# A three-layer graph network on one core: four record slots, pairs of tiles transposed with their numbers, features stored once

## The chip, the cores and the metric

The kernel runs on one core of a Trainium2 chip. The metric is the device time of one execution in microseconds (us); lower is better. The median of three runs of the kernel before is 3841.99 us.

## The reference, cut to what matters

```python
def reference(x, src, dst, edge_attr_16, We1, We2, Wn1, Wn2):
    # N, D, EF, L = 3125, 128, 16, 3 ; 100000 edges, each used in both directions
    s2, d2 = concatenate([src, dst]), concatenate([dst, src])
    ef2 = concatenate([ef, ef])
    h_prev = nf
    for l in range(L):
        e_in = concatenate([h_prev[s2], h_prev[d2], ef2], axis=-1)
        msg = leaky_relu(e_in @ We1[l]) @ We2[l]
        red = segment_sum(msg, d2, num_segments=N)
        n_in = concatenate([h_prev, red], axis=-1)
        out = leaky_relu(n_in @ Wn1[l]) @ Wn2[l]
        h_prev = out + h_prev
    return layernorm(x + out)
```

Each edge carries 16 features. Both directions of an edge share them.

## The kernel before

Three stages follow one another.

**Sort (0 to about 1122 us).** The edges are sorted by pairs of node blocks and written to the DRAM tensor `records`: 1152 tiles of 128 records, each of 34 float16 words (16 feature high halves, 16 low halves, and 2 numbers, the places of the edge's two nodes in their blocks).

**Reading the sorted records (about 1124 to 1284 us).** A batch is 32 tiles (`BATCH`), and two batches make one turn of the loop; 15 turns, so 30 batches, are live. `recc` has two slots, one for each batch of a turn. For a batch,
- GpSimd loads 272 KB of records into a slot (L644), once the batch two before it has been finished (`numT_set`, waited for at L643);
- TensorE transposes the features of each tile by itself (L1240: 32 transposes, 128x32 into 32x128, in four groups of eight, each to a bank of PSUM), and then the numbers of all 32 tiles in one more transpose (L1245);
- ScalarE copies two of the four groups to SBUF (L719) and VectorE the other two (L1018), 32x1024 each; VectorE also copies the numbers out of the records (L1011, L1013) and out of the last transpose (L1022). The copies of a batch with an even number go to `numb`, of an odd one to `gsel`, both free at this time;
- SyncE writes the features to the DRAM tensor `feat_d` twice (L529, two DMAs of 32 rows of 8 KB), so that it has 64 rows, and the numbers to `nums_d` (L532, 64 rows of 256 bytes).

At the end SyncE waits for these writes, copies the first part behind the last (L537, L538), and loads the first numbers and features of the next stage (L542, L546).

**Three layers (1319 to 2151, 2209 to 2970, 3025 to 3786 us).** Each runs 26 turns of 4 parts, a part is 3 steps, a step is 3 tiles. For each tile TensorE multiplies a tile of features (`fchunk`) with the weights `wst` (L1298), adds gathered node rows by four products with the one-hot matrix `gsel` (L1305), and after three steps adds the message to the sums by four products with `ssel`, a part of `loop_buf` (L1367, 12 for a step). ScalarE copies from PSUM (L750, L755) and makes the high half (L759); VectorE applies leaky relu (L1031) and makes the low half (L1101). In layer 0 VectorE also makes the one-hot matrices (L1035, L1118), and SyncE stores them to `gsel_d` and `ssel_d`; the other layers load them from there. There are 104 parts in a layer.

What sets the order around the change is SyncE's program, which issues one DMA after another:
- layer 0, for part p: wait until the gathers of the parts before p are done; load `fchunk` for part p+1 (L546: one DMA, 64 rows of 2304 bytes); wait for the one-hot matrix of part p+1; load numbers (L542), store `gsel` (L564), wait for the last `ssel` of part p, store it (L567);
- layers 1 and 2, for part p: wait until the sums of the steps before part p are done (`sum_done`); load `fchunk` for part p+1 (L546), `gsel` for part p+1 (L575), `ssel` for part p (L577).

TensorE waits in the first step of a part: for `fchunk` ahead of the first tile's feature product, for `gsel` ahead of its gathers, and for the `ssel` of the part before ahead of the third tile's feature product. `ssel` is thus loaded during the part just before the one that needs it.

`fchunk` rows 64 to 127 and `wst` rows 64 to 127 are set to zero once (L1037, L1038); `wst` is made anew in each layer (L1073 to L1079).

Of the kernel before, what the change touches and what calls it, by code (L numbers as in the profile page):

```python
# [23 lines left out]
P = 128  # L24
# [9 lines left out]
CHUNK = 8  # L34
# [8 lines left out]
TILES = 1152  # L43
# [7 lines left out]
assert TILES % (2 * BATCH) == 0  # L51
# [48 lines left out]
def build(nc, x, src, dst, ef, We1, We2, Wn1, Wn2, c_iota, c_part, c_tri, c_ident, c_tiles, c_steps, c_below, out):  # L100

    records = nc.dram_tensor("records", [TILES * P, RW], F16)
    feat_d = nc.dram_tensor("feat_d", [4 * EF, (TILES + PART) * P], F16)
# [8 lines left out]
    with ExitStack() as ctx:  # L112
# [105 lines left out]
        featT = [half[0:2 * EF, :, :].rearrange("p h e -> p (h e)")[:, 0:BATCH * P] for half in (numb, gsel)]  # L218
# [33 lines left out]
        recc = sb("recc", [P, 2, PREP, CHUNK, RW], F16)  # L252
        hrow = recc[:, :, :, :, :].rearrange("p k h t f -> p (k h t f)")[:, 0:2 * RUN * P].rearrange("p (h e) -> p h e", h=2)
        num16 = sb("num16", [P, 2, 2 * BATCH], F16)
        numT = sb("numT", [2 * BATCH, 2, P], F16)
# [17 lines left out]
        wc = sb("wc", [4 * EF, D], F32)  # L273
        wcs = sb("wcs", [4 * EF, D], F32)
        wch = sb("wch", [4 * EF, D], F16)
        wst = sb("wst", [P, 2, D], F16)
# [74 lines left out]
        recc_in = [sem(f"recc_in{h}") for h in range(2)]  # L351
        num16_set = sem("num16_set")
# [3 lines left out]
        numT_set = sem("numT_set")  # L356
        feat_out = [sem(f"feat_out{h}") for h in range(2)]
        nums_out = [sem(f"nums_out{h}") for h in range(2)]
# [58 lines left out]
        EDGE_DMAS, NODE_DMAS = 6, 2  # L417
# [26 lines left out]
        NUM_AHEAD = 2  # L444
        HIST_AHEAD = 2
        TR_STEPS = PREP + 1
# [4 lines left out]
        def _(sp):  # L451
# [11 lines left out]
            def load_edge_weights(l):  # L463
                sp.dma_start(wab[:, :, :], We1[ds(l, 1), 0:2 * D, :].rearrange("a (s k) f -> k (a s) f", s=2))\
                  .then_inc(w_in, DMA)
                for r in range(4):
                    sp.dma_start(wc[r * EF:(r + 1) * EF, :],
                                 We1[ds(l, 1), 2 * D:2 * D + EF, :].rearrange("a k f -> (a k) f")).then_inc(w_in, DMA)
# [14 lines left out]

            for h in range(2):
                sp.dma_start(feat_d[h * EF:(h + 1) * EF, TILES * P:TILES * P + RW], blank[0:EF, 0, :]).then_inc(feat_out[h], 16)
                sp.dma_start(nums_d[TILES * 2 + h * PREP:TILES * 2 + (h + 1) * PREP, 0:RW], blank[0:PREP, 0, :])\
                  .then_inc(nums_out[h], 16)
# [34 lines left out]
            with sp.Fori(0, PLOOPS) as it:  # L522
                with sp.If(it < live_p):
                    for k in range(2):
                        batch = it * 2 + k
                        sp.wait_ge(featA_set, batch * 2 + 2 + AHEAD)
                        sp.wait_ge(featD_set, batch * 2 + 2 + AHEAD)
                        for r in range(2):
                            sp.dma_start(feat_d[r * 2 * EF:(r + 1) * 2 * EF, ds(batch * (BATCH * P), BATCH * P)], featT[k])\  # L529
                              .then_inc(feat_out[k], 16)  # L530
                        sp.wait_ge(numT_set, batch + 1 + NUM_AHEAD)
                        sp.dma_start(nums_d[ds(batch * (2 * BATCH), 2 * BATCH), :], numT[:, k, :]).then_inc(nums_out[k], 16)  # L532
            for k in range(2):
                sp.wait_ge(feat_out[k], live_p * 32 + 16)
                sp.wait_ge(nums_out[k], live_p * 16 + 16)

            sp.dma_start(feat_d[:, ds(live_n * (ITER * P), PART * P)], feat_d[:, 0:PART * P]).then_inc(wrap_out, 16)  # L537
# [7 lines left out]
            def load_features(c, h):  # L545
                sp.dma_start(fchunk[0:4 * EF, h, :], feat_d[:, ds(c * (PART * P), PART * P)]).then_inc(fchunk_in[h], DMA)  # L546
# [4 lines left out]
            with sp.Fori(0, L) as l:  # L551
                with sp.Fori(0, TURNS) as it:
                    with sp.If(it < live_n):
                        with sp.If(l < 1):
                            for p in range(PARTS):
# [3 lines left out]
                                load_features(part_n + 1, 1 - h)  # L559
# [9 lines left out]
                        with sp.If(l > 0):  # L569
                            for p in range(PARTS):  # L570
# [3 lines left out]
                                load_features(part_n + 1, 1 - h)  # L574
# [78 lines left out]
        def _(act):  # L653
            for s in (featA_set, o_set, x_set):
                act.sem_inc(s, AHEAD)
# [874 lines left out]
```

## Time and profile before

| | |
|---|---|
| median of 3 runs | 3841.99 us (3841.14 to 3844.13) |
| the profiled execution | 3845.63 us, span of its instructions 3843.8 us |
| TensorE matmul | 2487.5 us busy, 65% |
| TensorE weight load | 2149.4 us, 56% |
| VectorE | 2776.0 us, 72% |
| ScalarE | 2124.5 us, 55% |
| GpSimd | 776.4 us, 20% |
| chain that ended last | TensorE 45%, DMA 11%, VectorE 6% |
| moved by DMA | 566.31 MB, mean 147 GB/s |

The shares are means over stages with different limits, so each stage is read by itself. The slices of the page show them: until slice 12 of 40 VectorE and GpSimd work (the sort), slices 12 and 13 hold the reading of the records, and from slice 14 TensorE is nearly full, with three short dips between the layers. A DMA-issuing instruction on SyncE's queue is written SPq; its duration is that of the issue, and "to landing" is from issue to the semaphore.

### The profile page before, as it was taken

The page shows a single profiled execution, that of the slowest core. Times are in us where ns is not written, and L with a number is a line of the kernel's source. Part 1 is how long each engine was busy: PE and PEld are TensorE (multiplying, and loading weights), DVE is VectorE, ACT ScalarE, POOL GpSimd, SP SyncE. Part 2 cuts the span into 40 slices and gives each one's busy share as a digit, 9 for nine tenths or more (in the row PEclk, how much of TensorE's full clock was granted, in tenths as well). Part 3 has the DMA queues.
Part 4 walks back from the last instruction along what each step waited for, and adds up shares of the span by engine and source line. Part 5 has one row for each costly group of instructions (what it writes and reads, how often), then busy time and mean ns, then how long its engine had stood idle before and what let it go on. Part 6 is the DMA issues. An engine that isn't in the chain of part 4 may idle for free.

```text
span 3843.8 us, 81410 instructions
## 1 busy us (share of the span) xinstructions
PE 2487.5 (65%) x27206; PEld 2149.4 (56%) x27207; DVE 2776.0 (72%) x3367; ACT 2124.5 (55%) x4171; POOL 776.4 (20%) x826
## 2 busy tenths in 40 slices
PE   4000000000015589999999699999999799999996
PEld 4000000000015577777777488888888588888884
DVE  8965565566423699999999677777777677777775
ACT  4000000000003577777777578888888688888884
POOL 0577777777751000000000000000000000000000
PEclk9555555555557799999999899999999899999998
DMA  8111111111026467777677345555554255555553
GB/s 240 55 41 32 43 43 31 43 43 31 16 45 158 116 232 242 244 240 239 240 243 240 132 165 181 181 181 182 188 180 168 88 182 190 180 180 186 183 182 109
DMA packets 202979, 566.31 MB, mean 147 GB/s; under 512 B 38553, under 2 KB 79839, under 8 KB 200895
## 3 DMA queue, kind: packets, MB, share of 16 engines
q1 hardware_dynamic: 175390, 550.42, 43.0%
q0 software_dynamic: 27552, 15.37, 2.1%
q8 instruction: 27, 0.44, 0.0%
q14 instruction: 10, 0.07, 0.0%
HBM read 407.88 MB, written 157.93 MB: 147 GB/s over the span
## 4 chain that ended last, share of the span: by engine, by line
PE 45%; DMA 11%; DVE 6%; issue 5%; SPq 2%; ACT 1%; POOL 0%; DVEq 0%; ACTq 0%; POOLq 0%
PE gath L1305 16%; PE sums L1367 11%; DMA fchunk<-feat_d 8%; PE sums L1305 8%; PE gath L1298 4%; PE sums L1298 2%; DMA recc<-records 2%; DVE big L1031 2%; PE sums L1240 1%; DVE loop_buf L1101 1%; DVE gsel L1035 1%; ACT big L755 1%; SPq L542 1%; PE sums L1465 1%; PE sums L1260 1%
## 5 line engine op out<-in xcount | busy, mean ns | idle before, releaser
L1031 DVE SCALAR_TENSOR_TENSOR big<-big 128x768 f32<-128x768 f32 (+1 forms) x957 | 909.5, 951 | 479.4 <-ACT big L755 437.8
L1305 PE MATMUL gath<-table,gsel 128*128 x7488 | 1079.0, 273 | 0.0
L1101 DVE TENSOR_TENSOR loop_buf<-big,loop_buf 128x768 f16<-128x768 f32 x936 | 891.2, 952 | 0.0
L630 POOL DMA_INDIRECT records<-rec,rowi x784 | 750.7, 958 | 284.6 <-issue 247.3
L1367 PE MATMUL sums<-loop_buf 128*128 128x128 f16 x11232 | 782.3, 219 | 29.0 <-issue 25.8
L1305 PEld LDWEIGHTS gath<-table,gsel 128*128 128x128 f16 x7488 | 734.6, 98 | 85.0
L759 ACT ACTIVATE loop_buf<-big 128x768 f16<-128x768 f32 x936 | 782.0, 835 | 0.0
L1367 PEld LDWEIGHTS sums<-loop_buf 128*128 128x128 f16 x11232 | 649.1, 98 | 125.3 <-ACT sums L753 36.9
L755 ACT ACTIVATE big<-gath 128x512 f32<-128x512 f32 x936 | 559.6, 598 | 283.8 <-PE gath L1305 283.8
L1221 PE MATMUL sums<-table,fchunk 128*128 128x200 f16 x196 | 37.1, 365 | 877.1 <-DVE found L944 864.6
L1305 PE MATMUL sums<-table,gsel 128*128 x3744 | 564.5, 274 | 0.8 <-DMA gsel<-gsel_d 0.4
L1221 PEld LDWEIGHTS sums<-table,fchunk 128*128 128x128 f16 x196 | 24.7, 136 | 889.2 <-issue 886.8
L1298 PE MATMUL gath<-wst,fchunk 128*128 128x256 f16 x1872 | 512.1, 274 | 4.1 <-DMA loop_buf<-ssel_d 0.2
L704 ACT ACTIVATE rec<-big,sc_ef 128x448 f16 x28 | 18.7, 669 | 881.0 <-DMA records<-rec,rowi 881.0
L750 ACT ACTIVATE big<-sums 128x256 f32<-128x256 f32 x936 | 353.6, 378 | 180.1 <-PE sums L1305 179.7
L1305 PEld LDWEIGHTS sums<-table,gsel 128*128 128x128 f16 x3744 | 367.0, 98 | 34.4 <-DVE gsel L1035 0.8
L753 ACT ACTIVATE sums<-iota 128x256 f32<-128x256 f16 x936 | 363.0, 388 | 29.5
L1298 PE MATMUL sums<-wst,fchunk 128*128 128x256 f16 x936 | 257.0, 275 | 154.0 <-issue 93.6
L650 POOL PARTITION_ALL_REDUCE mxa<-mx x3 | 1.1, 357 | 1730.9 <-DVE mx L1052 1730.9
L965 DVE SCALAR_TENSOR_TENSOR rowi<-rowb,rowc 128x28 int32<-128x28 int32 x28 | 5.3, 188 | 326.2 <-DMA records<-rec,rowi 325.9
L1298 PEld LDWEIGHTS gath<-wst,fchunk 128*128 128x128 f16 x1872 | 183.4, 98 | 43.3 <-issue 17.1
L1240 PE MATMUL sums<-ident,recc 128*32 128x128 f16 x960 | 87.7, 275 | 185.1 <-DMA recc<-records 176.5
(175 smaller groups left out, 1868.5 us busy)
## 6 DMA issues: line engine op xcount, KB each, us to landing
gsel<-gsel_d SPq DMA_DIRECT2D x208, 576.0 KB, 3.8
loop_buf<-ssel_d SPq DMA_DIRECT2D x208, 576.0 KB, 5.3
numb<-nums_d SPq DMA_DIRECT2D x106, 576.0 KB, 4.7
gsel_d<-gsel SPq DMA_DIRECT2D x104, 576.0 KB, 5.6
ssel_d<-loop_buf SPq DMA_DIRECT2D x104, 576.0 KB, 6.5
fchunk<-feat_d SPq DMA_DIRECT2D x313, 144.0 KB, 3.0
loop_buf<-rows_d SPq DMA_DIRECT2D x28, 896.0 KB, 4.8
records<-rec,rowi POOLq DMA_INDIRECT x784
```

The source lines that it names most:

```text
L630: pool.indirect_dma_start(out=records[:, :], out_offset=bass.IndirectOffsetOnAxis(ap=rowi[:, h, g:g + 1].bitcast(U32), axis=0), in_=rec[:, ...
L750: act.activation(msg[:, place, 0:2 * D], gath6, ACT.Copy).then_inc(x6_set, 1)
L753: act.activation(gath6, iota[:, 0:2 * D], ACT.Copy, scale=0.0).then_inc(gath6_free, 1)
L755: act.activation(msg[:, place, 2 * D:MSG], gath[:, :], ACT.Copy).then_inc(x_set, 1)
L759: act.activation(m_hi[:, (q - 1) % RING, :], msg[:, (q - 1) % RING, :], ACT.Copy)\
L1031: return dve.scalar_tensor_tensor(m, m, SLOPE, m, ALU.mult, ALU.max)
L1101: dve.tensor_tensor(m_lo[:, place, :], msg[:, place, :], m_hi[:, place, :], ALU.subtract)\
L1221: last = pe.matmul(sums[:, q * 2 * P:q * 2 * P + 2 * CHAINS * NB], oat[:, h, q * P:(q + 1) * P], bases[:, h, q, :, :, :].rearrange("p k r ...
L1240: last = pe.transpose(bank(h)[0:2 * EF, t * P // 2:(t + 1) * P // 2].bitcast(F16), recc[:, k, h, t, 0:2 * EF], ident16[:, :])
L1298: pe.matmul(uv, fchunk[:, h, tc * P:(tc + 1) * P], wst[:, :, :].rearrange("p s f -> p (s f)"), start=fresh, stop=False, skip_group_check=True)
L1305: return pe.matmul(uv, gsel[:, h, (2 * tc + s) * P:(2 * tc + s + 1) * P], at[n], start=False, stop=n == 3, skip_group_check=True)
L1367: last = pe.matmul(sum_at[i, s], m[:, place, w0:w0 + D], ssel[:, ts, s, :], start=False, stop=False, skip_group_check=True)
```

## The change

The records are read in four slots in place of two; the loop makes half as many turns, each with four batches in two halves. GpSimd's load waits until the batch four before it has been transposed.

TensorE transposes two tiles at once, with their numbers: 16 transposes for a batch, 128x68 into 68x128, to eight banks used in turn (the eighth is `gath`), so the copies have two batches' time before a bank is needed again. Rows 0 to 33 hold the even tile of a pair (32 features, 2 numbers), rows 34 to 67 the odd one. The copies are 68x512, two on each engine. The single transpose of numbers and two of VectorE's copies go away.

SyncE writes one DMA of 68 rows of 4096 bytes to `feat_d`, which is now [2, 34, pairs x 128], and two DMAs to `nums_d`, one for the even and one for the odd tiles, each of 2 x 16 rows of 256 bytes. A buffer is used again when all three have landed.

`fchunk` is loaded by four DMAs of 32 rows of 1280 bytes (5 pairs of tiles): even features, odd features, and both again. All 128 rows are in use, and a pair of tiles shares its 128 columns. `wst` gets a version for each side with zeros at the other side's rows, so that the feature product keeps its shape. Everything that waits for `fchunk` counts four DMAs. The weights of the features are loaded eight times in place of four.

```diff
             with sp.Fori(0, PLOOPS // 2) as it:
                 for half in range(2):
                     with sp.If(it * 2 + half < live_p):
                         for k in range(2):
                             batch = it * SLOTS_IN + half * 2 + k
-                        for r in range(2):
-                            sp.dma_start(feat_d[r * 2 * EF:(r + 1) * 2 * EF, ds(batch * (BATCH * P), BATCH * P)], featT[k])\
-                              .then_inc(feat_out[k], 16)
-                        sp.wait_ge(numT_set, batch + 1 + NUM_AHEAD)
-                        sp.dma_start(nums_d[ds(batch * (2 * BATCH), 2 * BATCH), :], numT[:, k, :]).then_inc(nums_out[k], 16)
+                            sp.wait_ge(featA_set, batch * 2 + 2 + BANK_AHEAD)
+                            sp.wait_ge(featD_set, batch * 2 + 2 + BANK_AHEAD)
+                            sp.dma_start(feat_d[:, :, ds(batch * (PAIR_COLS * P), PAIR_COLS * P)].rearrange("a f e -> (a f) e"),
+                                         recT[k]).then_inc(rec_out[k], 16)
+                            for a in range(2):
+                                sp.dma_start(nums_d[ds(batch * (2 * BATCH), 2 * BATCH), :]
+                                             .rearrange("(q a s) e -> a s q e", a=2, s=2)[a],
+                                             recT[k][a * RW + 2 * EF:(a + 1) * RW, :].rearrange("s (q e) -> s q e", e=P))\
+                                  .then_inc(rec_out[k], 16)
...
-            def load_features(c, h):
-                sp.dma_start(fchunk[0:4 * EF, h, :], feat_d[:, ds(c * (PART * P), PART * P)]).then_inc(fchunk_in[h], DMA)
+            def load_features(turn_n, p):
+                pair = (turn_n + p // PARTS) * ITER_PAIRS + p % PARTS * PART // 2
+                for r in range(2):
+                    for a in range(2):
+                        at = (2 * r + a) * 2 * EF
+                        sp.dma_start(fchunk[at:at + 2 * EF, p % 2, 0:PART_PAIRS * P],
+                                     feat_d[a:a + 1, 0:2 * EF, ds(pair * P, PART_PAIRS * P)].rearrange("a f e -> (a f) e"))\
+                          .then_inc(fchunk_in[p % 2], DMA)
...
+                            pool.wait_ge(tr_done, (batch + 1 - SLOTS_IN) * PREP + TR_AHEAD)
+                            pool.wait_ge(numcol_set, batch + 1)
...
+                                act.wait_ge(tr_done, batch * PREP + h + 1 + TR_AHEAD)
+                                act.wait_ge(rec_out[k], (it * 2 + (half + 1)) * (16 * OUT_DMAS))
+                                act.activation(recT[k][:, h * CHUNK // 2 * P:(h + 1) * CHUNK // 2 * P],
+                                               tr_bank(k, h)[0:2 * RW, 0:CHUNK // 2 * P // 2].bitcast(F16), ACT.Copy)\
+                                   .then_inc(featA_set, 1)
...
+                                for t in range(0, CHUNK, 2):
+                                    last = pe.transpose(tr_bank(k, h)[0:2 * RW, t * P // 4:(t + 2) * P // 4].bitcast(F16),
+                                                        recc[:, slot, h, t:t + 2, :].rearrange("p t f -> p (t f)"), ident16[:, :])
...
-            dve.memset(fchunk[4 * EF:P, :, :], 0.0)
-            dve.memset(wst[4 * EF:P, :, :], 0.0).then_inc(halves_zero, 1)
+            dve.memset(wst[:, :, :, :], 0.0).then_inc(halves_zero, 1)
...
+                for side in range(2):
+                    high, low = 2 * EF * side, 4 * EF + 2 * EF * side
+                    both = lambda w: w.unsqueeze(1).to_broadcast([2 * EF, 2, D])
+                    dve.tensor_copy(wst[high:high + 2 * EF, side, :, :], both(wch[high:high + 2 * EF, :]))
+                    dve.tensor_tensor(wst[low:low + 2 * EF, side, :, :], both(wcs[low:low + 2 * EF, :]),
+                                      both(wch[low:low + 2 * EF, :]), ALU.subtract).then_inc(wst_set, 1)
```

## Rows read from the trace of the kernel before

**Rows 1.** Busy times by window: reading the records, then the three layers.
```profile
core 0: us, PE busy (x) PEld busy (x) DVE busy (x) ACT busy (x) POOL busy (x), PEclk, DMA share, GB/s
1127.80:1283.20 155.40, 93.99 (x990) 85.52 (x991) 51.72 (x150) 57.53 (x60) 20.93 (x28) 0.73 0.64 151
1319.00:2151.60 832.60, 751.28 (x8424) 646.22 (x8424) 784.59 (x1064) 635.59 (x1248) 0.00 (x0) 0.99 0.70 237
2209.00:2970.40 761.40, 732.01 (x8424) 647.47 (x8424) 570.16 (x624) 624.80 (x1248) 0.00 (x0) 1.00 0.52 180
3025.00:3786.40 761.40, 731.06 (x8424) 647.01 (x8424) 570.15 (x624) 624.82 (x1248) 0.00 (x0) 1.00 0.52 180
```
**Rows 2.** The chain in order of time (start, length, what), one pair of batches.
```profile
1169.36 5.23 DMA recc<-records
1174.90 3.13 PE sums L1240 x32
```
**Rows 3.** The same chain from the last stored numbers to the first layer.
```profile
1283.63 3.00 DMA nums_d<-numT
...
1287.69 2.23 DMA nums_d<-nums_d
...
1305.37 0.28 DVE wst L1079
```
**Rows 4.** One line's instructions with durations (ns min/median/max): ScalarE's copies.
```profile
L719 ACT ACTIVATE gsel<-sums x30: 997/1005/1013, 1133.0 to 1280.2; 32x1024 f16<-32x1024 f16 x30
```
**Rows 5.** Queues of the DMA engines, 1130 to 1280 us (28 loads of records).
```profile
q1 hardware_dynamic: 5092, 15.68, 48.3%
q0 software_dynamic: 2240, 7.80, 18.2%
```
**Rows 6.** The end of the program: its last store, and windows as in rows 1.
```profile
out<-big SPq DMA_DIRECT2D x1, 26.5 KB
...
3841.50:3842.50 1.00, 0.00 (x0) 0.00 (x0) 0.00 (x0) 0.00 (x0) 0.00 (x0) 0.50 0.06 18
```
**Rows 7.** A window of layer 1 with full DMA engines.
```profile
2580.74:2581.74 1.00, 1.00 (x12) 0.83 (x10) 1.00 (x2) 0.83 (x3) 0.00 (x0) 1.00 1.01 401
```
**Rows 8.** Layer 0: waits (total us, times, longest), the DMA issues, the landing.
```profile
PE sums L1298 <- DMA fchunk<-feat_d: 60.3, 85, 3.0
...
1413.33 0.36 SPq L542 DMA_DIRECT2D numb<-nums_d  x1
...
1414.31 0.38 SPq L567 DMA_DIRECT2D ssel_d<-loop_buf  x1
1414.96 1.33 SPq L546 DMA_DIRECT2D fchunk<-feat_d  x1
...
1414.96 6.45 DMA fchunk<-feat_d
```
**Rows 9.** Layer 1, one part: TensorE's feature products and SyncE's issues.
```profile
2577.74 0.27 PE L1298 MATMUL sums<-wst,fchunk 128*128 128x256 f16 x1
...
2578.09 0.48 SPq L546 DMA_DIRECT2D fchunk<-feat_d  x1
2578.78 0.42 SPq L575 DMA_DIRECT2D gsel<-gsel_d  x1
2579.31 0.36 SPq L577 DMA_DIRECT2D loop_buf<-ssel_d  x1
...
2584.66 0.27 PE L1298 MATMUL sums<-wst,fchunk 128*128 128x256 f16 x1
...
2585.76 0.27 PE L1298 MATMUL gath<-wst,fchunk 128*128 128x256 f16 x1
```
**Rows 10.** Landing of L577: all 100 loads from 2230 to 2960 us, then one part's.
```profile
DMA to landing us min/median/max: 4.4/5.1/7.3
...
DMA to landing us min/median/max: 5.8/5.8/5.8
```
**Rows 11.** DMA issues with 32 rows: four in a row (1.88 us), and L529.
```profile
118.09 1.88 SPq L501 DMA_DIRECT2D recc<-rows_d  x4
...
L529 SPq DMA_DIRECT2D feat_d<-gsel x30: 314/318/333, 1135.4 to 1283.1; - x30
```

More of the change, by code:

```diff
@@ L216, in early @@
             return gsel_words[:, taken[0] - words:taken[0]]
-        featT = [half[0:2 * EF, :, :].rearrange("p h e -> p (h e)")[:, 0:BATCH * P] for half in (numb, gsel)]
+        recT = [half[0:2 * RW, :, :].rearrange("p h e -> p (h e)")[:, 0:PAIR_COLS * P] for half in (numb, gsel)]
         key16 = early(COLS // 2).bitcast(F16)
@@ L465, in load_edge_weights @@
                   .then_inc(w_in, DMA)
-                for r in range(4):
+                for r in range(P // EF):
                     sp.dma_start(wc[r * EF:(r + 1) * EF, :],
@@ new lines, in _ @@
+            with dve.Fori(0, PLOOPS // 2) as it:
+                for half in range(2):
+                    with dve.If(it * 2 + half < live_p):
+                        for k in range(2):
+                            slot = half * 2 + k
+                            batch = it * SLOTS_IN + slot
+                            dve.wait_ge(recc_in[slot], it * 16 + 16)
+                            dve.tensor_copy(numcol[:, ds(batch * (2 * BATCH), 2 * BATCH)].rearrange("p (t s) -> p t s", s=2),
+                                            recc[:, slot, :, :, 2 * EF:RW].rearrange("p h t s -> p (h t) s")).then_inc(numcol_set, 1)
+                            for h in range(2, PREP):
+                                dve.wait_ge(tr_done, batch * PREP + h + 1 + TR_AHEAD)
+                                dve.wait_ge(rec_out[k], (it * 2 + (half + 1)) * (16 * OUT_DMAS))
+                                dve.tensor_copy(recT[k][:, h * CHUNK // 2 * P:(h + 1) * CHUNK // 2 * P],
+                                                tr_bank(k, h)[0:2 * RW, 0:CHUNK // 2 * P // 2].bitcast(F16)).then_inc(featD_set, 1)
@@ L1247, in _ @@
-            pe.wait_ge(featA_set, live_p * 4 + AHEAD)
-            pe.wait_ge(featD_set, live_p * 4 + AHEAD)
-            pe.wait_ge(numT_set, live_p * 2 + NUM_AHEAD)
+            with pe.Fori(0, PLOOPS // 2) as it:
+                for half in range(2):
+                    with pe.If(it * 2 + half < live_p):
+                        for k in range(2):
+                            slot = half * 2 + k
+                            batch = it * SLOTS_IN + slot
+                            pe.wait_ge(recc_in[slot], it * 16 + 16)
+                            for h in range(PREP):
+                                if h % 2 == 0:
+                                    pe.wait_ge(featD_set if h else featA_set, batch * 2 - 2 + BANK_AHEAD)
+                                    pe.sem_inc(pe_go, 1)
+                                for t in range(0, CHUNK, 2):
+                                    last = pe.transpose(tr_bank(k, h)[0:2 * RW, t * P // 4:(t + 2) * P // 4].bitcast(F16),
+                                                        recc[:, slot, h, t:t + 2, :].rearrange("p t f -> p (t f)"), ident16[:, :])
+                                last.then_inc(tr_done, 1)
```

163 lines of the change are left out of this document (67 added, 96 removed).

## The prediction

> **What bounds the kernel now.** I read the page's slices first, to cut the span into stages, and then the busy times by window for the stages that the change touches [rows 1]. There are four: 155.4 us for reading the records, and three layers of 832.6, 761.4 and 761.4 us. The sort before them is left alone (four tiny blank stores go away there; SyncE waits later for TensorE in any case).
>
> Reading the records: no engine is full. Of 155.4 us TensorE is busy 94, ScalarE 58, VectorE 52, the DMA engines 0.64 [rows 1]. The chain shows what is late: a load of records of 5.2 us, then 3 to 3.6 us of transposes, and so on [rows 2]. A slot is loaded only after the batch two before it is finished, so with two slots each pair of batches pays the load and the transposes one after the other. 155.4/30 = 5.18 us for a batch.
>
> Layer 0: VectorE is busy 785 of 833 us, and TensorE waits 60.3 us, 85 times for 104 parts, for `fchunk` [rows 1, 8]. Its DMA is issued as the fourth of a burst and lands 6.45 us later, behind 1.7 MB of others.
>
> Layers 1 and 2: TensorE is busy 732 of 761 us [rows 1], and waits for no DMA but once or twice. That makes the slack of the DMAs the question. In the part of [rows 9] TensorE begins at 2577.74; SyncE issues `fchunk` at 2578.09, `gsel` at 2578.78, `ssel` at 2579.31, 1.57 us into the part. TensorE needs this `ssel` for the third feature product of the next part, at 2585.76, 8.02 us after the start. `ssel` lands 5.1 us after its issue at the median and 5.8 in this part [rows 10], that is at 6.7 to 7.4. So the slack is only 0.6 to 1.35 us, while the part takes 2584.66 - 2577.74 = 6.92 us.
>
> **The change part by part.** *Slots, pairs and copies.* With four slots a load has three batches' time; 16 transposes take half of 3.1 to 3.6 us [rows 2], so 1.8; ScalarE's two copies take half as many columns each, some 0.55 us of the 1005 ns [rows 4], so 1.1 in all. All engines would do 2 to 2.3 us a batch, and SyncE's three issues at about 0.5 to 0.7 us are 2 as well [rows 9, 11]. What is late next is the store, since a buffer is free again only when its three DMAs have landed.
>
> *The store of 68 rows.* The last store of the program has 53 rows of 512 bytes (26.5 KB). It runs at a DMA share of 0.06, one engine of sixteen, at 18 GB/s [rows 6], while stores and loads of 128 rows fill all sixteen (share 1.01, 401 GB/s, 25 GB/s for each) [rows 7]. Rows are thus not dealt out freely: 53 has no divisor up to 16, and goes on one engine; counts that sixteen divides go on sixteen. 68 is 4 x 17, so I take four engines. Each gets 17 rows of 4096 bytes: 17 x 4096/25 GB/s = 2.8 us. The two stores of numbers have an outer count of 2, so two engines, 32 rows of 256 bytes each in all: half to all of the 28 ns that a row of 512 bytes takes at 18 GB/s, 0.5 to 0.9, taken 0.6. The loads of records take 18.2% of 150 us for 28 loads on every engine [rows 5], 1.0 us. The two busiest engines need 2.8 + 0.6 + 1.0 = 4.4 us for a batch. The loop over a buffer agrees: copies 1.1 + hand-over 0.4, a small DMA's 2.2 us [rows 3] and the same 4.4, 8.1 us for two batches. So 4.4 takes the place of 5.18: 30 x 0.78 = -23 us. The last store, and the copy of the first part behind the last (68 rows, too), land later, on the path to the first numbers [rows 3]: +3. In all -20; with 3.9 us a batch -38, with 5.1 nothing. On sixteen engines the store would be 278 KB at 401 GB/s, 0.7 us, the loop 5.4 us for two, 2.7 a batch: -74.
>
> The Trainium skill, "DMA: Bandwidth & Descriptors", section "Why a DMA increments its semaphore by 16 and not by 1", says that a DMA uses the largest number of engines up to 16 that divides the slowest dimension of both sides. By it 68 rows go on 4 engines, 53 on 1, and the numbers on 2; the 53 rows agree.
>
> *`wst` and fills.* Four small VectorE instructions for each layer as before, twice as wide; one of them is 0.28 us now [rows 3]. At most +1 us in all; the fill of `fchunk` that goes away lay in a wait for numbers. The four more loads of weights have the whole node update between layers as cover. The feature product keeps its shape, so TensorE pays nothing.
>
> *`fchunk` by four DMAs, layer 0.* The burst holds the DMA engines long after the issue: `fchunk` lands 8 us after the burst's first issue at 1413.33 [rows 8]. The three more issues fit into that. Its bytes grow from 144 to 160 KB and its rows from 64 to 128: +0.1 to 0.3 us. A late `fchunk` delays the one-hot matrix that SyncE waits for before the burst after it, and that loop spans two parts: 52 loops x 0.2 = +10 us. Bounds: 0, and 52 x 1 us if the issue (1.33 us here, held up behind the burst) is held up each time.
>
> *Layers 1 and 2.* `gsel` and `ssel` stand behind `fchunk` in SyncE's program. Four DMAs of 32 rows in a row take 1.88 us, so (1.88 - 0.32)/3 = 0.52 from one to the next [rows 11]. Three more are 1.56; the 32-row issue is 0.16 shorter than 0.48 [rows 9]: `ssel` is issued 1.4 us later, at 2.97 us. It is in time if it lands within 8.02 - 2.97 = 5.05 us. With single landings spread evenly from 4.6, a little above the shortest, to 5.8 the mean lateness is 0.75 x 0.75/2/1.2 = 0.23, and I take 0.25 since the median of 5.1 lies above the bound. A late `ssel` delays the sums, and these start the next part's loads, so each lateness stays: 208 parts x 0.25 = +52 us. If an issue of 32 rows costs 0.69 as the present one of 64 does [rows 9], `ssel` is 2.07 later, 0.8 late in nearly every part: +150 us. Below: 0, if the landings get shorter once the loads stand apart.
>
> The Trainium skill, "SBUF — State Buffer", section "Summary: rules for kernel authors", advises one DMA and not several, and its section "The DMA setup-cost knee" gives each a fixed cost of about 2 us. If these followed one another, three more would make `ssel` 6 us later, an estimate by that page of over 1000 us for 208 parts. The trace disagrees for DMAs issued together: `gsel` and `ssel` are issued 0.53 us apart and both land within the part. I leave it out.
>
> Sum: -20 + 1 + 10 + 52 = +43 us on the profiled execution's 3845.6, so 3889; that execution is 3.6 above the median: 3885 us.
>
> **The rivals.** *A: SyncE's extra issues cost nothing* in layers 1 and 2. For it: at the shortest landing of 4.4 nothing is late. Against: the median of 5.1. -20 + 1 + 10 = -9: 3833 us. *B: the store runs on sixteen engines.* Only the row of 53 speaks against it. -74 + 1 + 10 + 52 = -11: 3831 us. A and B together: 3779 us. *C, slower still: each `fchunk` issue costs as much as now.* It decides above 1.8 us of delay, when nearly every `ssel` is late. For it: the issue of 0.48 us today; against: the 32-row issues of 0.32. -20 + 1 + 10 + 150 = +141: 3983 us.
>
> **How the numbers follow.** Forecast 58% (its own range 3855 to 3925), A 15%, B 12%, A and B 3%, C 12%. The range of 3812 to 3960 leaves out most of C, A and B together, and the fast tails of A and B, some 18%. 0.2% is 7.7 us, about what a measurement of this kernel tells from no change. Faster: half of A, 60% of B, A and B together, and 3% of the forecast's: 21%. Same: 12%. Slower: 67%.
>
> **What would show it.** The reading of the records should take 4.4 us a batch, with TensorE waiting for its copies and these for the store, and the DMA share at about 0.4 with two engines full; 2.7 a batch would be B. In layers 1 and 2 a new wait of TensorE for `ssel_d`'s load at the third feature product of a part, some 50 us in all, the part at 7.2 us; none would be A, 150 us C. In layer 0 a wait for `fchunk` longer by some 10 us. I am wrong altogether if the issues or the landings of the four loads move in another way than the rows of today show.

## The result and the profile after

The changed kernel took 3852.2 us (median of 9 runs, 3848.8 to 3859.1), the kernel before 3841.1 us in the same sessions: ratio 1.0032, 95% interval 1.0022 to 1.0043. It is slower by 11 us, 0.3%. Forecast were 3885 us and +43: the sign is right, the size is four times too large. The profiled execution has a span of 3847.8 us, 4.0 more than that of before; the stages below add up to this 4.0, and the other 7 are scatter: the profiled execution of before lies 4.5 us above its median, that of after 2.7 below. (Three experiments, `a5_both`, `b6_pool` and `a8_two_pool`, had some disturbed executions on the chip; only the undisturbed ones count for these.)

The first view is the busy times by window of the changed kernel, the same stages as in [rows 1]: reading the records, layers 0, 1 and 2.

```profile
core 0: us, PE busy (x) PEld busy (x) DVE busy (x) ACT busy (x) POOL busy (x), PEclk, DMA share, GB/s
1127.80:1265.00 137.20, 57.09 (x483) 51.38 (x484) 27.34 (x92) 32.32 (x60) 22.25 (x30) 0.51 0.40 123
1302.80:2142.00 839.20, 750.94 (x8424) 646.01 (x8424) 784.96 (x1064) 635.55 (x1248) 0.00 (x0) 1.00 0.69 238
2201.60:2970.90 769.30, 735.51 (x8425) 645.95 (x8425) 570.07 (x624) 628.03 (x1250) 0.00 (x0) 1.00 0.52 180
3027.00:3793.80 766.80, 734.44 (x8424) 646.52 (x8424) 570.08 (x624) 627.50 (x1250) 0.00 (x0) 1.00 0.53 181
```

The work did shrink where it was meant to: while the records are read TensorE is busy 57 us in place of 94, ScalarE 32 in place of 58, VectorE 27 in place of 52. The stage itself shrinks by far less, and all three layers are longer. In the table a layer runs from its first feature product to the first product of its node update, so its bounds differ a little from those of the windows above. The sort before the reading, which the change leaves alone, ended later in the changed kernel's profiled execution: the first load of records is issued at 1127.5 us and not at 1124.1, the first store of features 1.2 us later than before.

| us, profiled executions | layer 0 begins | layer 0 | layer 1 | layer 2 | gaps and tail | span |
|---|---|---|---|---|---|---|
| before | 1319.3 | 839.4 | 760.8 | 759.4 | 164.9 | 3843.8 |
| changed | 1302.8 | 846.2 | 769.2 | 766.8 | 162.8 | 3847.8 |
| difference | -16.5 | +6.8 | +8.4 | +7.4 | -2.1 | +4.0 |
| forecast | -19 | +10 | \ | +52 for both | 0 | +43 |

Three of the four terms are nearly met. The miss is layers 1 and 2: +16 where +52 was forecast. Layers that run the same program differ by some us from one kernel to the next: layer 0 of the kernel before took 839.4, 837.4 and 835.3 us (`before`, `b4_three_more`, `b5_delay`), that of the changed kernel 846.2, 847.1, 844.7 and 844.3 us (`a1_store80`, `a2_two_more` and `a6_71` have it too).

**Reading the records.** The longest pieces of the chain that ended last, in order of time (start, length, what), one batch of the changed kernel:

```profile
1203.00 7.58 DMA nums_d<-gsel
1210.96 0.06 ACTq L740
1211.16 0.59 ACT gsel L742
1211.98 0.26 SPq L532
1212.44 0.24 SPq L535
```

Where loads of records and transposes stood in turn in [rows 2], there is now one loop: a store lands, ScalarE copies into the buffer that has come free, SyncE issues the next store. One time round is 8.9 us for two batches (the buffers `numb` and `gsel` alternate). The issues of L532 for all 30 batches run from 1133.5 to 1263.2 us: 129.7/29 = 4.47 us a batch, against the forecast's 4.4.

**Layer 0.** TensorE's longest wait, and **layer 1**, what is late there that hardly was before (total us, times, longest):

```profile
PE sums L1321 <- DMA fchunk<-feat_d: 66.7, 84, 3.0
```
```profile
PEld sums L1390 <- ACT sums L777: 7.2, 22, 0.7
PEld gath L1321 <- DMA loop_buf<-ssel_d: 3.5, 7, 1.0
```

In layer 0 the wait for `fchunk` grew by 6.4 us from the 60.3 of [rows 8], which is the layer's +6.8. In layer 1 the forecast's new wait is there, at the third feature product, 7 times (before: once, 0.5 us), and after it a second one that I had not named: TensorE loads weights later because ScalarE's copies of a disturbed step are late, 22 times for 7.2 us (before: 3 times, 0.9 us).

SyncE's issues in one part of layer 1, whose first feature product is at 2285.96, and below them the issues and landings of the whole layer (line, count, KB, median us to landing):

```profile
2286.32 1.78 SPq L557 DMA_DIRECT2D fchunk<-feat_d  x4
2288.29 0.35 SPq L588 DMA_DIRECT2D gsel<-gsel_d  x1
2288.73 0.39 SPq L590 DMA_DIRECT2D loop_buf<-ssel_d  x1
```
```profile
gsel<-gsel_d SPq DMA_DIRECT2D x103, 576.0 KB, 3.7
loop_buf<-ssel_d SPq DMA_DIRECT2D x103, 576.0 KB, 4.7
fchunk<-feat_d SPq DMA_DIRECT2D x412, 40.0 KB, 1.7
```

The four issues take 1.78 us. `ssel`'s load comes 2.77 us into the part (forecast 2.97, before 1.57), and it lands after 4.7 us where the loads of [rows 10] took 5.1. The second number is the one that the prediction had not moved.

### The profile page after: what moved, and what is told of

Its sections match the earlier page's. It is cut to its first block, busy times and chain, and to the rows that moved or that the text cites. A ratio compares the mean times of both kernels' runs of the same rounds, so it can differ in the third digit from the quotient of the medians.

```text
span 3847.8 us, 82375 instructions
## 1 busy us (share of the span) xinstructions
PE 2454.7 (64%) x26696; PEld 2111.8 (55%) x26697; DVE 2750.5 (71%) x3306; ACT 2103.5 (55%) x4171; POOL 779.0 (20%) x826
## 4 chain that ended last, share of the span: by engine, by line
PE 43%; DMA 8%; SPq 6%; DVE 6%; issue 6%; ACT 2%; POOL 0%; ACTq 0%; DVEq 0%; POOLq 0%
PE gath L1328 15%; PE sums L1390 11%; PE sums L1328 8%; SPq L557 5%; PE gath L1321 4%; DMA fchunk<-feat_d 4%; DMA nums_d<-gsel 2%; PE sums L1321 2%; DVE big L1053 2%; DVE loop_buf L1124 1%; DVE gsel L1057 1%; DMA loop_buf<-ssel_d 1%; ACT big L779 1%; DVE loop_buf L1141 1%; PE sums L1282 1%
## 5 line engine op out<-in xcount | busy, mean ns | idle before, releaser
L1321 PEld LDWEIGHTS sums<-wst,fchunk 128*128 128x128 f16 x936 | 91.4, 98 | 180.2 <-issue 98.6
```

The lines of the kernel that those rows point to most:

```text
L1321: pe.matmul(uv, fchunk[:, h, pair * P:(pair + 1) * P], wst[:, side, :, :].rearrange("p s f -> p (s f)"), start=fresh, stop=False, skip_gro ...
```

## The experiments

Labels beginning with a are edits of the changed kernel, with b of the kernel before. Each "+" below is against the profiled execution of the kernel before.

### Which step costs what: `a1_store80`, `a2_two_more`, `a3_pool`, `b4_three_more`

`a1_store80`: the feature store and its tensor in DRAM get 80 rows in place of 68 (12 rows of no use).

```
-    sp.dma_start(feat_d[:, :, ds(...)].rearrange("a f e -> (a f) e"), recT[k])     # 2 x 34 rows
+    sp.dma_start(feat_d[:, ds(...)], recT80[k])                                    # 80 rows
```

> The changed kernel with one edit: the feature store has 80 rows in place of 68 (the last 12 are filler that nothing reads), and feat_d 80 rows. Theory (a store of 68 rows goes on 4 DMA engines, one of 80 on 16, and the store is what the reading of the records waits for): the store's 17 rows for an engine become 5, its transfer 2.8 us becomes 0.8, a batch takes 2.5 to 3.4 us in place of 4.45, the reading of the records gets 30 to 58 us shorter, in all about 3800 us. Rival (the number of DMAs and their fixed time, or the stores of numbers on few engines, set the pace): still 4.3 to 4.5 us a batch, 3850 us.

Measured: 3808.3 us (ratio to before 0.9922, 0.9906 to 0.9939). Storing 18% more bytes took 44 us off. Layer 0 begins at 1256.1, 46.8 us earlier than in the changed kernel, 2.5 of them because the sort ended earlier; the layers are as in it (847.1, 771.0, 767.8). The same chain, its longest pieces over two batches:

```profile
1176.80 4.21 DMA nums_d<-numb
1181.53 0.59 ACT numb L744
1182.35 0.33 SPq L534
1183.30 4.12 DMA nums_d<-numb
```

The loop is 6.2 to 6.5 us for two batches and not 8.9, 3.1 us a batch. So the store's engines set the time of the reading, and rival B's mechanism (a store on sixteen engines) would have been worth most of the 54 us that it claimed beyond the forecast, had the store had another number of rows.

`a2_two_more`: two more loads (32 rows of 1280 bytes, to a spare buffer that nobody reads) ahead of `gsel`'s in layers 1 and 2 of the changed kernel. `b4_three_more`: three of them in the kernel before, between its one `fchunk` load and `gsel`'s.

```
+    for j in range(2):                      # 3 in b4_three_more
+        sp.dma_start(spare[:, j, :], feat_d[...32 rows of the part...]).then_inc(spare_in, 16)
     sp.dma_start(gsel[:, 1 - h, :], gsel_d[...])
```

> The changed kernel with two more loads of 32 rows x 1280 bytes (to a spare tile that nothing reads) issued between fchunk's four and gsel's, in layers 1 and 2. Theory (the slack of ssel was only just not used up by the four loads): ssel's load is issued 3.8 us into the part, lands 4.7 us later against a need at 8.0, so 0.5 us late in each of 208 parts: +80 to +120 us. Rival (the place of ssel's load in SyncE's program does not decide; landings shorten as it is issued later): within 20 us of the changed kernel.

> The kernel before with three more loads of 32 rows x 1280 bytes (to a spare tile that nothing reads) between fchunk's one load and gsel's, in layers 1 and 2. It has the delay of the changed kernel with the old form of fchunk. Theory 1 (landings of ssel get shorter, from 5.2 to 4.7 us, as soon as its load stands apart from fchunk's): +5 to +20 us, ssel's landing 4.7 us. Theory 2 (the shorter landings come from the new form of fchunk's loads): ssel's landing stays at 5.2 us at the median and the kernel gets 50 to 90 us slower.

Measured: `a2_two_more` 3942.5 us, 90 more than the changed kernel and within its range, layers 1 and 2 +57.6 and +52.3 (`ssel` issued 3.9 us into the part, landing 4.8). `b4_three_more` 3883.3 us, +23.0 and +22.9 (issued at 3.12 at the median, landing 4.8), with the records and layer 0 as before. Its landing is that of theory 1, but the 43 us that it costs lie above theory 1's range and below theory 2's. Each of the two is one execution. SyncE's issues of one part in `b4_three_more`:

```profile
2285.06 0.50 SPq L549 DMA_DIRECT2D fchunk<-feat_d  x1
2285.93 1.27 SPq L582 DMA_DIRECT2D spare<-feat_d  x3
2287.39 0.35 SPq L583 DMA_DIRECT2D gsel<-gsel_d  x1
2287.83 0.38 SPq L585 DMA_DIRECT2D loop_buf<-ssel_d  x1
```

More issues ahead of `ssel`, with `fchunk` as it was, make layers 1 and 2 longer, and steeply so: rival A (issues cost nothing) holds only up to a point shortly before where the changed kernel stands.

`a3_pool`: `fchunk`'s four loads are issued by GpSimd, which has nothing to do in the layers.

```
-    sp.dma_start(fchunk[at:at + 2 * EF, ...], feat_d[...]).then_inc(fchunk_in[p % 2], DMA)
+    pool.dma_start(fchunk[at:at + 2 * EF, ...], feat_d[...]).then_inc(fchunk_in[p % 2], DMA)
```

> The changed kernel with fchunk's loads issued by GpSimd in all three layers, at the same waits; SyncE keeps gsel, ssel and numbers. Theory (the cost of the change in the layers is SyncE's issues): layers 1 and 2 lose the 13 us that they gained; in layer 0 fchunk no longer lands behind the burst, the wait of 67 us goes and VectorE sets the pace: 20 to 40 us less there. In all 3800 to 3820 us. Rival (GpSimd's DMAs are slower to be issued beside a busy VectorE, or the loads collide with gsel and ssel in the DMA engines): no gain or slower than 3850 us.

Measured: 3826.5 us (ratio to before 0.9964, 0.995 to 0.9978), 26 less than the changed kernel. That is 6 us above the expected range: layer 0 is 829.4 (17 less, where 20 to 40 were expected), layers 1 and 2 are 763.7 and 764.9 (5.5 and 1.9 less, of 13 expected). `ssel` is issued 0.8 us into its part, but lands after 5.2 us.

### Do the gains add, and is GpSimd's queue only a repair: `a5_both`, `b6_pool`

> The changed kernel with both single edits that helped it: the feature store of 80 rows (alone 3808 us, reading the records 46.8 us shorter than in the changed kernel) and fchunk's loads issued by GpSimd (alone 3826 us; layer 0 17 us and layer 1 5 us shorter). They touch different stages, so if each works by the step I name (store: engines it is dealt to; GpSimd: SyncE's queue ahead of the part's other loads) the gains add: 3808 - 26 = 3782 us (3775 to 3795), start of layer 0 at about 1256 us, layer 0 about 830 us long. Rival: both gains come from one thing (less load on SyncE's queue or on the transfer engines in general), then they don't add and the time stays at 3805 us or above.

Measured: 3781.4 us with `a1`'s and `a3`'s edits together (ratio to before 0.9851, 0.9831 to 0.987). They add to a microsecond.

`b6_pool` has the one load of the kernel before issued by GpSimd.

> The kernel before, with its one fchunk load per part issued by GpSimd instead of SyncE. My theory: what a part of layers 1 and 2 pays for is when ssel's load is issued and lands; in the kernel before that already costs next to nothing, so layers 1 and 2 stay within 3 us each of 760.8 and 759.4 us, and ssel's offset in its part falls from 1.56 to about 0.9 us. In layer 0, whose wait for fchunk was 60.3 us, the load no longer queues behind the numbers' and ssel's, and 10 to 20 us go. In all 3820 to 3832 us, about 3825. If it comes out there, the four issues of the change cost only what stood on SyncE's queue. Rival: GpSimd's issues gained in the changed kernel only by undoing its four issues; then the kernel before gains nothing: 3836 to 3845 us, layer 0 unchanged at 839 us.

Measured: 3806.5 and 3811.8 us (ratio 0.9926, 0.9902 to 0.995), below the 3820 to 3832 that I expected. Layers 1 and 2 did what they should (759.4 and 759.1). Layer 0 fell by 32 us, to 807.5, and not by 10 to 20. The issues and landings there:

```profile
numb<-nums_d SPq DMA_DIRECT2D x104, 576.0 KB, 4.9
gsel_d<-gsel SPq DMA_DIRECT2D x104, 576.0 KB, 5.8
ssel_d<-loop_buf SPq DMA_DIRECT2D x104, 576.0 KB, 6.8
fchunk<-feat_d POOLq DMA_DIRECT2D x103, 144.0 KB, 3.7
```

From SyncE the same load landed after 6.3 us at the median; from GpSimd it lands after 3.7. One part's issues show why (first SyncE's, then GpSimd's):

```profile
1416.70 0.35 SPq L542 DMA_DIRECT2D numb<-nums_d  x1
1417.26 0.33 SPq L560 DMA_DIRECT2D gsel_d<-gsel  x1
1417.79 0.33 SPq L563 DMA_DIRECT2D ssel_d<-loop_buf  x1
```
```profile
1416.26 0.52 POOL L644 DMA_DIRECT2D fchunk<-feat_d  x1 [7.57 <-PE gath L1317]
```

The load is now issued 0.5 us ahead of the burst at the median, where in [rows 8] it was the burst's fourth: 0.15 us into the part at the median and not 1.7. It overtakes nothing; of its 103 loads in this layer none lands before a big transfer that was issued ahead of it. In SyncE's program it stands behind the wait for the last `ssel` of the part before, while GpSimd waits for the gathers alone. TensorE's wait for it (60.3 us) is gone from the list, and the longest named wait of the layer is 14.1 us for VectorE's one-hot matrices. So half the 60 us had been paid for the load's place in SyncE's program, in the kernel before already.

### How a store of 68 rows is dealt: `a6_71`

> The changed kernel with the feature store of 71 rows in place of 68 (80 rows took 46.8 us off). 71 rows have no divisor up to 16 but 1. Theory, that the number of transfer engines is the largest divisor of the rows up to 16: one engine takes all 71 rows of 4096 bytes; at the 18 GB/s that one engine moved in the end-of-program store of 53 rows that is 16 us a batch, at 25 GB/s (401 GB/s over 16 engines) 11.6 us, against the 4.4 us a batch now: reading the records 230 to 400 us longer at 32 full batches, total 4060 to 4250 us. Rival: the rows are dealt freely, and 80 rows helped for another reason (a store that doesn't cross its two halves); then 71 rows cost as 80 do, 3800 to 3815 us, or, if the count of rows itself is what matters, 3850 us as with 68.

Measured: 4179.1 us in one execution, whose sort, ahead of the edited stage, was itself some 68 us longer (GpSimd's scatters took 1027 ns each and not 961, and the first load of records is issued at 1195.6 us and not at 1127.5), so the stage must be read by itself. The store's issues into one of the two buffers run from 1309.1 to 1550.3 us for 10 rounds: 24.1 us for two batches, 12.06 for one.

```profile
1330.09 14.15 DMA nums_d<-gsel
1353.80 14.75 DMA nums_d<-gsel
1378.73 14.15 DMA nums_d<-gsel
1395.54 6.72 SPq L537
```

71 rows of 4096 bytes in 12.06 us are 24.1 GB/s: one engine of sixteen at the rate of [rows 7]. Three more rows made the batch 2.7 times as long, and twelve more made it a third shorter. Neither bytes nor rows explain this; divisors do (68: 4, 71: 1, 80: 16). The trace's records of single packets show it directly. In this stage, of the time in which the store's packets of 4096 bytes are on their way, they go one at a time for 98% with 71 rows, and at most four at a time for 97% with 68 rows; with 80 rows it is up to sixteen, 8.3 at the mean. The last row shows a by-product: the issues of the stores of numbers, 0.24 to 0.25 us at the median with 80 rows, take 3.7 to 4.0 us here, 7.1 at most. That the one engine's queue was full is my reading of it, not tested.

The Trainium skill, "DMA: Bandwidth & Descriptors", section "Why a DMA increments its semaphore by 16 and not by 1", gives this rule. The three counts agree with it.

### Why `ssel` landed sooner than forecast: `b5_delay`

24 semaphore increments on SyncE between the loads of `fchunk` and `gsel`, in the kernel before: time without a transfer.

```
+    for _ in range(24):
+        sp.sem_inc(sp_go, 1)
     sp.dma_start(gsel[:, 1 - h, :], gsel_d[...])
```

> The kernel before, with 24 semaphore increments on SyncE between fchunk's load and gsel's in each part of layers 1 and 2: a delay of some 1 to 1.5 us without any transfer. It puts ssel's load at 2.6 to 3.1 us after its part's start, as in the changed kernel (2.76) and as with three more loads (3.1). Theory: ssel's landing falls from 5.2 to 4.7 or 4.8 us because its load no longer coincides with fchunk's; then layers 1 and 2 together cost 10 to 45 us more, by the delay as with the changed kernel (+14 at 2.76) and with three more loads (+44 at 3.1). Rival: landing is shorter only where the feature load is split or is followed by short loads; then ssel's landing stays at 5.1 to 5.3 us and, at the same offset, layers 1 and 2 cost about 50 us or more already at 2.76. In layer 0 nothing changes (839 us).

Measured: 3871.7 us, layers 1 and 2 +13.9 and +13.4, layer 0 835.3. One part's issues (its first feature product is at 2282.05), and the landing of all `ssel` loads of layer 1:

```profile
2282.39 0.51 SPq L546 DMA_DIRECT2D fchunk<-feat_d  x1
2284.52 0.34 SPq L577 DMA_DIRECT2D gsel<-gsel_d  x1
2284.96 0.38 SPq L579 DMA_DIRECT2D loop_buf<-ssel_d  x1
```
```profile
DMA to landing us min/median/max: 4.4/4.7/6.2
```

The landing fell from 5.1 to 4.7 us with the same transfers in the same order, only later. It isn't the split of `fchunk` that shortens it; it is that `ssel` no longer shares its first microseconds with `fchunk`'s load. The reverse is seen where GpSimd issues `fchunk` at about the moment of `ssel`: `ssel` lands after 5.4 us in `b6_pool`.

### Fewer issues: `a7_two_loads`, `a8_two_pool`, `a9_split`, `a10_split_pool`

`a7_two_loads` is `a1_store80` with each pair of `fchunk`'s loads (32 rows each) made one of 64 rows, which lie in DRAM as two groups of 32 out of 34; `a8_two_pool` issues them on GpSimd.

```
+    sp.dma_start(fchunk[r * 4 * EF:(r + 1) * 4 * EF, ...],
+                 feat_d[0:2 * RW, ...].rearrange("(a f) e -> a f e", a=2)[:, 0:2 * EF, :])
```

> The changed kernel with the store of 80 rows (3808 us), and fchunk's four loads of 32 rows in each part made into two loads of 64 rows, all still issued by SyncE. It takes two issues of some 0.35 us from each part. Theory, that layers 1 and 2 pay by when ssel's load is issued: its offset falls from 2.76 to about 2.1 us, and of the 10 to 14 us that the two layers cost above the kernel before most go (layer 1 at 761 to 765 us); layer 0, 847 us, falls by 0 to 7 us. In all 3788 to 3802 us, about 3795. Rival: what costs is the data's way (each feature row fetched twice a part, more and shorter packets), not the number of issues: then layers 1 and 2 stay at 769 to 771 us each and the time at 3804 to 3810 us.

> The changed kernel with all three edits: store of 80 rows, fchunk's loads issued by GpSimd, two of them in place of four. With four (3781 us) GpSimd's issues took 0.52 us each and TensorE still waited for fchunk for 8.1 us in layer 1 and 13.6 us in layer 2. Theory: with two, fchunk lands 1 us earlier in its part, those waits go (layers 1 and 2 at 759 to 762 us each, 9 to 13 us in all), and layer 0 goes from 829 us some way towards the 807.5 us of the kernel before with one GpSimd load, to about 818: 3755 to 3773 us, about 3763. Rival: in the kernel with four the waits for fchunk are of the transfers and not of the issues; then it stays at 3778 to 3783 us.

Measured: 4252.3 us and 3889.5 us; in both kernels both expectations, mine and the rival's, missed by far. `a7`'s layers were 1026.7, 903.4 and 905.3 us long. In its layer 1:

```profile
gsel<-gsel_d SPq DMA_DIRECT2D x103, 576.0 KB, 7.6
loop_buf<-ssel_d SPq DMA_DIRECT2D x103, 576.0 KB, 8.6
fchunk<-feat_d SPq DMA_DIRECT2D x206, 80.0 KB
```

Each load of the two behind them lands 3.9 us later than in the changed kernel. The outermost dimension of the source is 2 there. If the load runs on two engines, as the rule about divisors says, each gets 40 KB of each `fchunk` load, 1.6 us at 25 GB/s, 3.3 us for both, and `gsel` and `ssel` wait behind them on these two engines. The packet records bear this out: in layer 1 `fchunk`'s packets go at most two at a time for 82% of their time, and for 36% of theirs `gsel`'s and `ssel`'s packets go at most two at a time, too (18% and 6% in `a9_split` below). I had used this very rule for the store and hadn't applied it to my own edit. In `a8_two_pool`, where GpSimd issues the two loads, nothing behind them is held up (`gsel` lands after 3.8 us, `ssel` after 5.1), but the second `fchunk` load lands 7.5 us into its part, after the next part would begin (6.92), and TensorE waits for it: layers 0 to 2 are 855.9, 806.0 and 803.6 us.

`a9_split` tests that: the features are stored by two stores of 32 rows a batch, from the two row groups, into a tensor of 64 rows; a `fchunk` load then reads 64 rows as one run. `a10_split_pool` issues these loads on GpSimd.

```
+    for a in range(2):
+        sp.dma_start(feat_d[a * 2 * EF:(a + 1) * 2 * EF, ds(...)], recT[k][a * RW:a * RW + 2 * EF, :])
...
+    for r in range(2):
+        sp.dma_start(fchunk[r * 4 * EF:(r + 1) * 4 * EF, p % 2, ...], feat_d[:, ds(pair * P, PART_PAIRS * P)])
```

> The changed kernel with its feature rows stored by two stores of 32 rows a batch (in place of one of 68), so that the 64 feature rows lie together in DRAM, and a part's features read by two loads of 64 rows seen as one run of rows, issued by SyncE. With the same two loads from 68 rows, seen as 2 by 32 rows, the time was 4252 us (TensorE waited 137.7 us for fchunk in layer 0, and ssel landed after 8.6 us in place of 4.7). Theory, that a transfer's engines are the largest divisor up to 16 of the slowest dimension of the view, which was 2 there: now it is 64, 16 engines, so fchunk lands in 1.7 to 2.9 us and ssel in 4.7; the 32-row stores go over 16 engines, so reading the records is as short as with 80 rows (layer 0 starts at 1256 to 1262 us), and with two issues less a part layers 1 and 2 come to 761 to 765 us each: 3785 to 3800 us, about 3793. Rival: it is the two larger loads themselves (80 KB in place of 40 KB each) that held up ssel: then the time stays above 4100 us.

> As the split store with two loads of 64 rows, with fchunk's loads issued by GpSimd. The kernel before with one load issued by GpSimd had layer 0 at 807.5 us and layers 1 and 2 at 759.4 and 759.1 us; the changed one with four had 829 us, 765 and 766 us. Theory: with two loads layer 0 comes out between, 812 to 822 us, layers 1 and 2 at 759 to 762 us each, and the start of layer 0 at 1256 to 1262 us: 3752 to 3772 us, about 3762. Rival: TensorE's waits for fchunk are of the transfer and of VectorE's and GpSimd's contention and not of the number of issues: then 3778 to 3785 us, as with four loads.

Measured: `a9_split` 3774.2 us (ratio to before 0.9833, 0.9816 to 0.9849) and `a10_split_pool` 3749.0 us (0.9765, 0.9748 to 0.9781). The same two loads a part as in `a7_two_loads`, only with the rows in one run, make the kernel 478 us faster; the stores of the reading differ too, but layer 0 begins only 5 us earlier (1251.9 and 1257.2), so nearly all of it lies in the layers. `a9`'s layer 1, then the windows of `a10_split_pool` (reading, layers 0, 1, 2):

```profile
gsel<-gsel_d SPq DMA_DIRECT2D x103, 576.0 KB, 4.0
loop_buf<-ssel_d SPq DMA_DIRECT2D x103, 576.0 KB, 4.8
fchunk<-feat_d SPq DMA_DIRECT2D x206, 80.0 KB, 2.3
```
```profile
1127.00:1219.00 92.00, 55.91 (x492) 50.24 (x493) 29.39 (x95) 33.36 (x62) 19.83 (x27) 0.58 0.69 178
1251.90:2059.00 807.10, 751.35 (x8423) 641.79 (x8420) 776.21 (x1064) 638.86 (x1255) 107.57 (x206) 0.99 0.76 249
2112.30:2874.00 761.70, 731.89 (x8424) 647.29 (x8424) 570.10 (x624) 625.51 (x1250) 107.29 (x206) 1.00 0.53 182
2932.30:3693.10 760.80, 732.13 (x8424) 648.28 (x8424) 570.09 (x624) 624.96 (x1250) 107.29 (x206) 1.00 0.53 182
```

`a10_split_pool` beats the kernel before by 2.3%: 68 us of it in the reading, 31 in layer 0, nothing in layers 1 and 2. Both came out below their expected range, by 11 and by 3 us: layer 0 begins 4 to 5 us before the expected 1256, and it is shorter (836.4 and 808.5); against `a1_store80` it is 10.7 us shorter in `a9_split`, which has two issues less in a part. The reading is now 3.0 us a batch (store issues in `a9_split` from 1129.8 to 1216.6, 29 batches), where 2.7 had been estimated for sixteen engines.

## Why the prediction was right or wrong

**The store, -20: right.** 4.47 us a batch for 4.4, and four engines for 68 rows. From the store's first issue to its last it takes 21.0 us less; the first is 1.2 us later, so the last is 19.9 us earlier. From there to the first product of layer 0 it takes 3.4 us longer, for which the forecast had +3 and +1. In all -16.5 results. The term was built from one row about a store of 53 rows, and `a1_store80` and `a6_71` bear it out from both sides.

**Layer 0, +10: right in kind and size** (+6.8, all of it in the wait for `fchunk`). What the prediction missed is that the whole of that wait was open to gain: it took the load's place in SyncE's program as given, and `b6_pool` got 32 us out of it.

**Layers 1 and 2, +52: the step that failed.** The failed step is the mean lateness of 0.25 us a part. The path was right: the cost goes with how late `ssel` is. The landings that were put into it were wrong, 5.1 us at the median and spread from 4.6 to 5.8. This table has seven of the kernels in order of `ssel`'s issue, at medians of layer 1. Late by the prediction's own bound is what lies above 8.02 us after the part's start.

| kernel | `ssel` issued, us into the part | landing, median | sum | layer 1 | layer 2 |
|---|---|---|---|---|---|
| `b6_pool` | 0.8 | 5.4 | 6.2 | -1.4 | -0.3 |
| before | 1.57 | 5.1 | 6.7 | 0 | 0 |
| `a9_split` | 2.2 | 4.8 | 7.0 | +0.7 | +1.1 |
| changed | 2.77 | 4.7 | 7.5 | +8.4 | +7.4 |
| `b5_delay` | 2.9 | 4.7 | 7.6 | +13.9 | +13.4 |
| `b4_three_more` | 3.12 | 4.8 | 7.9 | +23.0 | +22.9 |
| `a2_two_more` | 3.9 | 4.8 | 8.7 | +57.6 | +52.3 |

In these seven the cost rises with the sum, whatever stood between the loads. Their order by issue alone is the same, so they don't tell the two apart. Two more kernels have the changed kernel's layers and its issue at 2.77: `a1_store80` with +10.2 and +8.4, and `a6_71`, in its one execution, with +13.2 and +14.5. A difference of a few us between neighbours in the table is thus no more than scatter.

The forecast's sum was 2.97 + 5.1 = 8.07, and it came out 0.6 us lower. A third of this (0.2 us) is the issues: (1.78 - 0.36)/3 = 0.47 us from one to the next and not 0.52, and `ssel`'s 0.44 behind `gsel`'s and not 0.53. Two thirds (0.4 us) are the landings, 4.7 and not 5.1. I had taken them from [rows 10], where `ssel`'s load starts 1.2 us after `fchunk`'s. The change that delays the load also ends that overlap, and the prediction names this ("if the landings get shorter once the loads stand apart") but keeps it as the lower end only. The spread narrowed, too: of the 103 landings of layer 1 five lie above 8.02 - 2.77 = 5.25 us, while in the kernel before 48 do.

**A second step was wrong the other way.** The forecast let each us of lateness cost one us. By its bound the late landings of the changed kernel add up to 4 us in the two layers (2.0 and 2.3), and the layers grew by 16. In `b4_three_more`, whose bound is 8.02 - 3.12 = 4.90 us, they add up to 10 us (4.5 and 5.0), and the layers grew by 46. With the issues and landings as measured, and its own price, the forecast would have been +4 and not +52. That its +52 for a sum of 8.07 looks so near to the +46 at 7.9 is luck: too much lateness at too low a price.

**What stays open.** Why a late `ssel` costs several times its lateness. In layer 1 of the changed kernel TensorE's waits for `ssel` are 3.5 us and the layer grew by 8.4. The rest goes along with the waits for ScalarE's copies (7.2 us, 22 times), as if one late step upset several after it. No run took that apart.

**Two slips in the prediction's sums.** Rival C's 0.8 us in 208 parts are 166 us and not 150, and the named shares of "faster" add up to 19% and not 21%. Nothing hangs on either.

**GpSimd's queue has its own price.** In `a3_pool` and `a5_both` `ssel` is early (sum 6.0), and yet layers 1 and 2 are 3 to 7 us longer than before. In `a5_both` TensorE's weight loads wait for `fchunk` there (5.2 us in layer 1, 8.5 in layer 2): four issues of GpSimd are 2.1 us (0.52 each), and the loads land 4.5 us after issue. With two, in `a10_split_pool`, +1.0 and +1.4 remain.

**The rivals.** A was wrong by degree: the issues cost 16 us and not nothing, but much less than I gave them. B was false for 68 rows and true for 80. C was false: a 32-row issue costs less than one of 64 rows.

The Trainium skill, "SBUF — State Buffer", section "Summary: rules for kernel authors", advises one DMA and not several for a transfer that DMA bounds. The runs agree with its direction: two loads in place of four went with 10.7 us less in layer 0 and 17 less in layers 1 and 2 together (`a9_split` against `a1_store80`: 771.0 - 761.5 and 767.8 - 760.5). But what a part pays per DMA is the 0.47 us of its issue, and that only once the slack behind it is used up. `a7_two_loads` is the counterexample: fewer DMAs and 444 us slower than `a1_store80`.

## What to carry to other kernels

Before costing a DMA by its bytes, write down the outermost count of both of its views and its largest divisor up to 16: padding a store from 68 to 80 rows or splitting it into 32 and 32 can be worth more than the rewrite around it, and a view of 2 by 32 rows can cost 12% of a kernel. When a load is moved in time, don't carry its landing over from the old place: say what it overlapped with there, and give both landings a chance. And look at what a small load that someone waits for stands behind in its engine's program: if that is a wait it doesn't need, an engine with nothing to do can issue it earlier.

## What the runs showed of the hardware

- Engines of a store: 71 rows ran at 24.1 GB/s in all, one packet at a time (12.06 us a batch); 68 rows took 4.47 us a batch with at most four packets at a time, 80 rows 3.1 and twice 32 rows 3.0 with up to sixteen, with the rest of the loop alike.
- Two loads of 80 KB whose source was seen as 2 by 32 rows held up 576 KB loads behind them in SyncE's queue by 3.9 us; seen as 64 rows by 0.3 us and 0.1 us (`gsel` 4.0 and not 3.7, `ssel` 4.8 and not 4.7 us). Issued by GpSimd, the 2 by 32 rows held up neither (3.8 and 5.1 us).
- A 576 KB load landed after 5.1 us when a load of 144 KB was issued 1.2 us ahead of it, after 4.7 us when it was 2.5 us ahead, and after 5.4 us when both were issued at about the same time from two queues.
- The `fchunk` load of layer 0 landed after 6.3 us when SyncE issued it behind three loads and stores of 576 KB, and after 3.7 us when GpSimd issued it 0.5 us ahead of them.
- GpSimd issued a load in 0.52 us (0.65 for the view of 2 by 32 rows), SyncE in 0.33 to 0.36 us for 32 rows. Where the store went to one engine SyncE's issues behind it took 3.7 to 4.0 us at the median, where it went to sixteen 0.24 to 0.25.
